# A feed-forward input turned by transposing transfers in place of TensorE's turns

## The chip, the cores and the metric

One core of one Trainium2 chip runs the whole program. The metric is the device time of one execution in microseconds (us). TensorE, VectorE, ScalarE and GpSimd work side by side, each following its own list of instructions and waiting on semaphores; transfers are issued from the queue of SyncE (SP).

## The reference, cut to what matters

The program computes one transformer layer: attention of x (4 x 2048 rows of 512) over a context of 4 x 154 rows, and then a quantised feed-forward part with a short convolution.

```python
x = x + xattn(layernorm(x), ctx)            # 16 heads of 32
h = bit_linear(layernorm(x), w1)            # act_quant of each row, ternary w1: 512 -> 2048
h = silu(depthwise_conv1d(h))               # 3 taps along the sequence
x = x + bit_linear(h, w2)                   # act_quant again, ternary w2: 2048 -> 512

def act_quant(x):
    scale = 127.0 / jnp.clip(jnp.max(jnp.abs(x), axis=-1, keepdims=True), 1e-05)
    return jnp.clip(jnp.round(x * scale), -128, 127) / scale
```

The change is about the input of the first `bit_linear`. Its rows are quantised with 128 sequence positions on the partitions, and the product with w1 needs the 512 channels there, so the quantised block must be turned (transposed).

## The kernel before

The 8192 rows are cut into 16 blocks of TB = 512 rows; a block is four tiles of P = 128 rows. Setup turns and splits the weights. Then 19 slots follow, numbered s = -1 to NB + 1 = 17 (`slots`, line 431). In slot s four blocks are under way: block s + 1 gets its first norm and queries (`do_q`), block s its attention, output projection, second norm and quantisation (`do_a`), block s - 1 its feed-forward part up to the quantised hidden layer (`do_f`), and block s - 2 its second product and result (`do_m`). Every engine's list is written out by hand in this order; there is no scheduler. "Slot 6" is s = 6, from about 595 to 680 us of the trace.

The step that changes stands at the end of a slot:

- ScalarE quantises the four tiles of block s (line 1522) into `osb`, as fp16 numbers; `hlq(i)` is the view of tile i, every second fp16 place of its 2 KB row. Each raises `xq_ok`.
- TensorE runs the 16 pieces of the query scores of block s + 1 (`query_scores`, line 1016). After each piece VectorE takes a maximum (line 1835); the banks alternate, so piece n waits for maximum n - 2. Between the pieces stand products of `mm2` (line 1085), and after pieces 13, 14 and 15 the turns `turn_xq` (line 1044): for each of four channel groups k, four transposes of 128 x 128 into half a PSUM bank (`xq_half`).
- ScalarE copies the four halves into `xqT` (line 1540), with the second copy of turned maxima `negmT` in between.
- TensorE turns the last maxima (line 1032), spreads the row of scales (`spread_row`, line 1053), and `mm1_ahead` (line 913) issues the first two products with w1 (line 891). The first of them waits for `xqc`, that is for the four copies. The next slot begins with the attention scores (line 854), which wait for the turned maxima that SP's queue brings into row 96 of `qs` (line 573, semaphore `m_in`).
- SP's list at the end of a slot: 12 transfers of the q parts (`qs<-hl`, line 558), two stores of border rows into `fx_scratch` (lines 565 and 566), two stores of results (line 511), the two transfers of turned maxima (line 573), each after its copy (`mtc`), two more stores of results, and then the load of x for a later slot (line 462).

In slot 15 there are no queries any more: the 16 turns stand together behind a part of `mm2(3)`, before the row of scales. `osb` is free for the next attention when the turns are over (line 1807), and for the border rows of the last step too (line 583).

Of the kernel before, what the change touches and what calls it, by code (L numbers as in the profile page):

```python
# [28 lines left out]
P = 128  # L29
# [9 lines left out]
def build(nc, x, ctx_in, Wq, bq, Wk, bk, Wv, bv, Wo, bo, w1, conv_w, conv_b, w2, out):  # L39
# [33 lines left out]
    with ExitStack() as ctx:  # L73
# [131 lines left out]

        def xq_half(s, k):

            bank = A[4] if k < 2 else A[5] if s == NB - 1 else F[0]
            return bank.bitcast(F16)[:, (k % 2) * TB:(k % 2 + 1) * TB]

        def row_bank(s):
# [11 lines left out]
        def hlq(i):  # L223

            return osb[:, i, :].bitcast(F16)[:, 0:2 * D:2]

# [94 lines left out]
        dgs_ok = sem("dgs_ok")  # L321
        xqt_ok = sem("xqt_ok")
        xqc = sem("xqc")
        sr_ok = sem("sr_ok")
# [121 lines left out]
        def _(sp):  # L446
# [59 lines left out]
            def slot(s, m, batch_of):  # L506
# [56 lines left out]
                if do_a:  # L563
                    sp.wait_ge(x2_ok, at(s, TT, TT))
                    sp.dma_start(fx_d[bass.ds(3 * s, 2), :], ring(s)[P - 2:P, TT - 1, :]).then_inc(fx_out[m % 2], 16)
                    sp.dma_start(fx_d[3 * NB:3 * NB + 1, :] if s == 0 else fx_d[bass.ds(3 * s - 1, 1), :],
                                 ring(s)[0:1, 0, :]).then_inc(fx_out[m % 2], 16)
                if do_m and do_a:
                    store_rows(range(2 if late_results(s) else TT))
# [10 lines left out]
                if s == NB:  # L580
                    for q in fx_out:
                        sp.wait_ge(q, 16 * NB)
                    sp.wait_ge(xqt_ok, KT * NB)
                    for bb in range(NBATCH):
# [110 lines left out]
        def _(pe):  # L695
# [135 lines left out]
            def slot(s, m, batch_of):  # L831
# [81 lines left out]
                def mm1_ahead(c):  # L913

                    if c == 0:
                        if s == 1:
                            pe.wait_ge(csum_ok, 1)
                        pe.wait_ge(xqc, at(s, KT, KT))
                        if do_m and s != NB - 1:
                            pe.wait_ge(out_ok, at(s, 4, 3 - 8))  # L920
                    if c == 1 and s == NB - 1:
                        pe.wait_ge(src, at(s, 1, 1))
                    mm1(c)

# [99 lines left out]
                def turn_maxima(tiles):  # L1024
# [8 lines left out]
                    r.then_inc(mt_ok, 1)  # L1033

                def turn_xq(ks):

                    for k in ks:
                        if k == 0:
                            pe.wait_ge(xq_ok, at(s, TT, TT))
                        if k == 2 and do_q:  # L1040
                            pe.wait_ge(mtc, at(s, 2, 3))
                        bank = xq_half(s, k)
                        for i in range(TT):
                            r = tp(bank[:, i * P:(i + 1) * P], hlq(i)[:, k * P:(k + 1) * P], identh[:])
                        r.then_inc(xqt_ok, 1)

# [124 lines left out]
                if s == NB - 1:  # L1171
                    mm2(2)
                    mm2(3, range(0, 11))
                    turn_xq(range(KT))
                    spread_row()
# [3 lines left out]
                for n in range(0 if s == NB - 1 else TT * NG):  # L1179
# [11 lines left out]
                    if do_q and n == 13:  # L1191
                        turn_maxima(range(0, TT - 1))
                    if do_a and n in (13, 14):
                        turn_xq((n - 13,))
                    if do_a and n == 15:
                        turn_xq((2, 3))
                if s == NB + 1:
# [22 lines left out]
        def _(act):  # L1220
# [73 lines left out]
            def slot(s, m, batch_of):  # L1294
# [242 lines left out]
                for k in range(KT):  # L1537
                    if do_a:
                        act.wait_ge(xqt_ok, at(s, KT, k + 2 - k % 2))
                        copy(xqT[:, k, :], xq_half(s, k)).then_inc(xqc, 1)  # L1540
                    if do_q and k == KT - 2:
# [15 lines left out]
        def _(dve):  # L1557
# [82 lines left out]
            def slot(s, m, batch_of):  # L1640
# [159 lines left out]
                def attention(k):  # L1800
# [5 lines left out]
                    elif k == 0:  # L1806
                        dve.wait_ge(xqt_ok, at(s, KT, 0))
                    dve.wait_ge(rz_ok, at(s, NG, k + 1))
# [238 lines left out]
```

## Time and profile before

| | us |
|---|---|
| median of 3 runs | 1520.56 (1520.53 to 1521.53) |
| the profiled execution | 1520.43 |
| its span, first to last instruction | 1518.6 |
| TensorE busy | 1460.6 (96%) |
| VectorE busy | 1278.0 (84%) |
| ScalarE busy | 1185.3 (78%) |
| GpSimd busy | 1028.7 (68%) |
| SP's queue, packets' share of 16 engines | 19.1% |

The profile is of one execution. Busy TensorE time is modelled from pipelined matmuls, each counted with its latency, so neighbours overlap and the share says less than it seems; which wait ended last is read from the timelines. In the rows PE is TensorE, DVE VectorE, ACT ScalarE, and SPq SP's queue; L1044 is line 1044 of the kernel. Copies on ScalarE all carry the line of the helper `copy`, L1222, and are told apart by their tiles. A row with x16 stands for 16 instructions merged, with the time from the start of the first to the end of the last.

### The profile page before, as it was taken

The numbers are of one execution on the slowest core, as the hardware profiler recorded it, in microseconds if no ns is written. First come the engines' busy times: TensorE is split into PE (matmuls) and PEld (weight loads), VectorE is DVE, ScalarE is ACT, GpSimd is POOL, SyncE is SP. The second block draws the span as 40 slices with busy tenths as digits, with TensorE's granted clock in tenths as the row PEclk, the third lists the DMA queues.
The fourth block names the chain that finished last, engine by engine and source line by source line (L and its number), as shares of the span: only waits on it lengthen the run. The fifth ranks groups of instructions, "written<-read, shape, count | busy, mean of one in ns | idle before, by whom it ended". The sixth has DMA issues, their size and how long they took to land. (4 is left out here: it accounts for less than half of the span.)

```text
span 1518.6 us, 24856 instructions
## 1 busy us (share of the span) xinstructions
PE 1460.6 (96%) x9102; PEld 892.5 (59%) x9102; DVE 1278.0 (84%) x2002; ACT 1185.3 (78%) x2190; POOL 1028.7 (68%) x834
## 2 busy tenths in 40 slices
PE   9998988999999999999999999999999999999898
PEld 6474655657575665657575665657575655656343
DVE  5787796898979889898979898897979898887877
ACT  3567788979787888979687888979687888978763
POOL 4011567868675977968675977968675877968543
PEclk8999899999999999999999999999999999999999
DMA  8561002021310303030310303030210202020001
GB/s 258 148 193 42 29 8 71 8 80 32 76 43 12 94 8 99 8 93 19 75 44 18 88 8 99 8 100 14 73 43 23 84 8 71 8 71 1 31 1 56
DMA packets 80343, 85.21 MB, mean 56 GB/s; under 512 B 29983, under 2 KB 55839, under 8 KB 79709
## 3 DMA queue, kind: packets, MB, share of 16 engines
q1 hardware_dynamic: 80221, 83.62, 19.1%
q8 instruction: 72, 1.18, 0.3%
q14 instruction: 50, 0.41, 0.1%
HBM read 38.74 MB, written 19.42 MB: 38 GB/s over the span
## 5 line engine op out<-in xcount | busy, mean ns | idle before, releaser
L675 POOL TENSOR_TENSOR h<-h,gall 128x512 f32<-128x512 f32 x233 | 343.9, 1476 | 18.3
L660 POOL TENSOR_TENSOR h<-h,r 128x512 f32<-128x512 f32 x240 | 307.0, 1322 | 52.5 <-ACT r L1222 50.6
L673 POOL TENSOR_TENSOR gall<-gall,cw 128x512 f32<-128x512 f32 x233 | 255.3, 1096 | 112.6 <-DVE h L1751 112.6
L1751 DVE SCALAR_TENSOR_TENSOR h<-gall,cw,h 128x512 f32<-128x512 f32 x249 | 253.2, 1020 | 47.6 <-ACT h L1320 47.4
L885 PEld LDWEIGHTS ps<-va,pexp 128*128 128x128 f32 x2048 | 259.5, 192 | 29.0 <-issue 10.9
L1676 DVE SCALAR_TENSOR_TENSOR gall<-ps,bias,srow 128x512 f32<-128x512 f32 x256 | 191.1, 747 | 94.3 <-POOL h L675 57.9
L891 PE MATMUL ps<-xqT,w1T 128*128 128x512 f16 x1024 | 255.1, 379 | 6.6 <-DVE gall L1676 6.5
L885 PE MATMUL ps<-va,pexp 128*128 128x33 f32 x2048 | 257.7, 270 | 0.0
L1085 PE MATMUL ps<-w2T,hqb 128*128 128x512 fp8e4 x960 | 242.4, 380 | 0.0
L1320 ACT ACTIVATE h<-gall,cb,cw 128x512 f32<-128x512 f32 x249 | 216.3, 869 | 8.3
L1301 ACT ACTIVATE pexp<-ps 128x512 f32<-128x512 f32 x320 | 179.8, 589 | 54.5 <-PE ps L854 27.9
L1835 DVE TENSOR_REDUCE negm<-ps 128x4 f16<-128x616 f32 x256 | 185.8, 793 | 20.3 <-PE ps L1016 15.0
L1222 ACT ACTIVATE hqb<-h 128x512 f16<-128x512 f32 x276 | 174.4, 683 | 36.0 <-POOL h L660 16.1
L710 PE MATMUL ps<-hl,WqT 128*128 128x512 f16 x768 | 170.8, 379 | 2.7 <-DVE hl L1793 2.6
L1339 ACT ACTIVATE h<-h 128x512 f32<-128x512 f32 x249 | 151.0, 688 | 12.3 <-POOL h L675 11.7
L997 PE MATMUL ps<-WoT,pexp 128*128 128x512 f16 x512 | 156.1, 382 | 1.7 <-DVE xn L1814 1.7
L891 PEld LDWEIGHTS ps<-xqT,w1T 128*128 128x128 fp8e4 x1024 | 101.8, 111 | 84.0 <-DVE gall L1676 8.9
L1085 PEld LDWEIGHTS ps<-w2T,hqb 128*128 128x128 f16 x960 | 92.5, 98 | 81.0 <-issue 3.9
L685 POOL TENSOR_TENSOR nw<-nw,mhalf 128x4 f32<-128x4 f32 x16 | 16.3, 1019 | 176.5 <-DVE nw L1845 176.5
L710 PEld LDWEIGHTS ps<-hl,WqT 128*128 128x128 f16 x768 | 74.1, 98 | 91.5 <-issue 8.0
L1016 PE MATMUL ps<-kB,hl 128*128 128x308 f16 x512 | 116.2, 305 | 11.5 <-DVE negm L1835 9.1
L1398 ACT ACTIVATE xn<-xr,sum 128x512 f32<-128x512 f32 x64 | 44.3, 717 | 78.0 <-DVE xr L1821 71.5
(226 smaller groups left out, 2336.8 us busy)
## 6 DMA issues: line engine op xcount, KB each, us to landing
qs<-hl SPq DMA_DIRECT2D x192, 128.0 KB, 2.4
xr<-in_x SPq DMA_DIRECT2D x16, 1024.0 KB, 5.4
out<-xr SPq DMA_DIRECT2D x64, 256.0 KB
h<-in_L_ffn_w SPq DMA_DIRECT2D x8, 1024.0 KB, 5.4
srow<-in_L_xattn_bo SPq DMA_DIRECT2D x15, 256.0 KB, 3.3
kst<-kh_scratch SPq DMA_DIRECT2D x32, 38.5 KB
xr<-in_ctx SPq DMA_DIRECT2D x1, 1024.0 KB
h<-in_L_xattn_Wk SPq DMA_DIRECT2D x1, 1024.0 KB, 8.2
```

What stands on the lines that cost most here:

```text
L660: gp.tensor_tensor(hc(c), hc(c), r2[:], ALU.mult).then_inc(u_ok, 1)
L673: gp.tensor_tensor(right, right, cw[:, c, 2:3].to_broadcast([P, TB]), ALU.mult).then_inc(c2m_ok, 1)
L675: gp.tensor_tensor(hc(c), hc(c), right, ALU.add).then_inc(c2p_ok, 1)
L710: r = mm(bank, a, b_, start=i == 0, stop=i == n - 1, **kw)
L885: r = mm(o, pr[:, t * P:(t + 1) * P], rhs, start=j == 0 and t % 2 == 0, stop=j == J, skip_group_check=True)
L891: r = mm(F[(c + 1) % 2], w1T[:, k, c * P:(c + 1) * P], xqT[:, k, :], start=k == 0, stop=k == KT - 1)
L1085: r = mm(bank, hq(c)[:, i * P:(i + 1) * P], w2T[:, c, :], start=False, stop=c == CT - 1, skip_group_check=late_results(s))
L1301: nc.scalar.activation(pexp[:, i % 3, :], A[i % 2], ACT.Exp, scale=1.0 / QS).then_inc(e_ok, 1)
L1320: nc.scalar.activation(hc(c), g[:, c % 4, 0:TB], ACT.Identity, bias=cb[:, c:c + 1], scale=cw[:, c, 0:1]).then_inc(c0_ok, 1)
L1676: ve.scalar_tensor_tensor(out=g[:, c % 4, 1:TB + 1], in0=F[(c + 1) % 2], scalar=bias1[:, c:c + 1], in1=srow[:], op0=ALU.add, op1=ALU.mult) ...
L1751: ve.scalar_tensor_tensor(out=hc(c), in0=g[:, c % 4, 1:TB + 1], scalar=cw[:, c, 1:2], in1=hc(c), op0=ALU.mult, op1=ALU.add).then_inc(c1_ok, 1)
L1835: ve.tensor_reduce(negm[:, i, k * J:(k + 1) * J].rearrange("p (b e) -> p b e", b=2), banks, AX.X, ALU.max, negate=True).then_inc(mx_ok, 1)
```

## The change

The four quantised tiles are turned by four transfers with `transpose=True`, issued on SP's queue in the slot of their block: transfer i waits for `xq_ok` of tile i and writes columns i * 128 to (i + 1) * 128 of all four channel groups of `xqT`. `turn_xq`, `xq_half`, the 64 copies and the semaphores `xqt_ok` and `xqc` are gone; `xq_turned` rises by 16 for each transfer. `hlq` is now a packed view. The first product waits for all four transfers, and the second one gets a wait for the first copy of turned maxima, which reads the bank that it writes.

```diff
--- before.py
+++ after.py
@@ -203,11 +203,6 @@
         def halves(bank, n):
             return bank.bitcast(F16)[:, 0:n]
 
-        def xq_half(s, k):
-
-            bank = A[4] if k < 2 else A[5] if s == NB - 1 else F[0]
-            return bank.bitcast(F16)[:, (k % 2) * TB:(k % 2 + 1) * TB]
-
         def row_bank(s):
 
             return F[0] if s == NB - 1 else A[2]
@@ -222,7 +217,7 @@
 
         def hlq(i):
 
-            return osb[:, i, :].bitcast(F16)[:, 0:2 * D:2]
+            return osb[:, i, :].bitcast(F16)[:, 0:D]
 
         def ah(k):
 
@@ -319,8 +314,7 @@
         pw2 = sem("pw2")
         xq_ok = sem("xq_ok")
         dgs_ok = sem("dgs_ok")
-        xqt_ok = sem("xqt_ok")
-        xqc = sem("xqc")
+        xq_turned = sem("xq_turned")
         sr_ok = sem("sr_ok")
         src = sem("src")
 
@@ -565,6 +559,10 @@
                     sp.dma_start(fx_d[bass.ds(3 * s, 2), :], ring(s)[P - 2:P, TT - 1, :]).then_inc(fx_out[m % 2], 16)
                     sp.dma_start(fx_d[3 * NB:3 * NB + 1, :] if s == 0 else fx_d[bass.ds(3 * s - 1, 1), :],
                                  ring(s)[0:1, 0, :]).then_inc(fx_out[m % 2], 16)
+                if do_a:
+                    for i in range(TT):
+                        sp.wait_ge(xq_ok, at(s, TT, i + 1))
+                        sp.dma_start(xqT[:, :, i * P:(i + 1) * P], hlq(i), transpose=True).then_inc(xq_turned, 16)
                 if do_m and do_a:
                     store_rows(range(2 if late_results(s) else TT))
                 if do_q:
@@ -580,7 +578,7 @@
                 if s == NB:
                     for q in fx_out:
                         sp.wait_ge(q, 16 * NB)
-                    sp.wait_ge(xqt_ok, KT * NB)
+                    sp.wait_ge(xq_turned, 16 * TT * NB)
                     for bb in range(NBATCH):
                         sp.dma_start(fxr[9 * bb:9 * bb + 9, :], fx_d[12 * bb:12 * bb + 9, :]).then_inc(fx_in, 16)
                         sp.dma_start(fx2[3 * bb:3 * bb + 3, :], fx_d[12 * bb:12 * bb + 9, :].rearrange("(m r) d -> m r d", r=3)[:, 1, :]
@@ -915,11 +913,13 @@
                     if c == 0:
                         if s == 1:
                             pe.wait_ge(csum_ok, 1)
-                        pe.wait_ge(xqc, at(s, KT, KT))
+                        pe.wait_ge(xq_turned, at(s, 16 * TT, 16 * TT))
                         if do_m and s != NB - 1:
                             pe.wait_ge(out_ok, at(s, 4, 3 - 8))
                     if c == 1 and s == NB - 1:
                         pe.wait_ge(src, at(s, 1, 1))
+                    if c == 1 and do_q:
+                        pe.wait_ge(mtc, at(s, 2, 3))
                     mm1(c)
 
                 def fix_turn():
@@ -1031,18 +1031,6 @@
                     for i in tiles:
                         r = tp(bank[0:H, i * P:(i + 1) * P], negm[:, i, :], identh[:])
                     r.then_inc(mt_ok, 1)
-
-                def turn_xq(ks):
-
-                    for k in ks:
-                        if k == 0:
-                            pe.wait_ge(xq_ok, at(s, TT, TT))
-                        if k == 2 and do_q:
-                            pe.wait_ge(mtc, at(s, 2, 3))
-                        bank = xq_half(s, k)
-                        for i in range(TT):
-                            r = tp(bank[:, i * P:(i + 1) * P], hlq(i)[:, k * P:(k + 1) * P], identh[:])
-                        r.then_inc(xqt_ok, 1)
 
                 def spread_row():
 
@@ -1171,7 +1159,6 @@
                 if s == NB - 1:
                     mm2(2)
                     mm2(3, range(0, 11))
-                    turn_xq(range(KT))
                     spread_row()
                     mm2(3, range(11, CT))
                     mm1_ahead(0)
@@ -1190,10 +1177,6 @@
                             mm2(3, MM2_LAST[n - 4])
                     if do_q and n == 13:
                         turn_maxima(range(0, TT - 1))
-                    if do_a and n in (13, 14):
-                        turn_xq((n - 13,))
-                    if do_a and n == 15:
-                        turn_xq((2, 3))
                 if s == NB + 1:
                     pe.wait_ge(out_ok, at(s, 4, 4 - 12))
                     for i in range(TT):
@@ -1535,9 +1518,6 @@
                         act.wait_ge(m_in, at(s, 32, 32))
                     copy(negmT[:, 0:LATE], halves(F[0], TB)[0:H, 0:LATE]).then_inc(mtc, 1)
                 for k in range(KT):
-                    if do_a:
-                        act.wait_ge(xqt_ok, at(s, KT, k + 2 - k % 2))
-                        copy(xqT[:, k, :], xq_half(s, k)).then_inc(xqc, 1)
                     if do_q and k == KT - 2:
                         act.wait_ge(mt_ok, at(s, 2, 4))
                         copy(negmT[:, LATE:TB], halves(A[0], TB)[0:H, LATE:TB]).then_inc(mtc, 1)
@@ -1804,7 +1784,7 @@
                         for q in v_out:
                             dve.wait_ge(q, 64)
                     elif k == 0:
-                        dve.wait_ge(xqt_ok, at(s, KT, 0))
+                        dve.wait_ge(xq_turned, at(s, 16 * TT, 0))
                     dve.wait_ge(rz_ok, at(s, NG, k + 1))
                     ve.tensor_tensor(osb[:, k, :].rearrange("p (u e d) -> p u e d", u=2, d=HD), opair(k)[:, :, :, 0:HD],
                                      rz[:, k].unsqueeze(3).to_broadcast([P, 2, 2 * J, HD]), ALU.mult).then_inc(at_ok, 1)
```

SP's queue at the end of slot 6, as its list stands before (`qs<-hl` are the q parts, `qs<-negmT` the turned maxima):

```order
L558 DMA qs<-hl 32x4x512 x12
L565 DMA fx_scratch<-xr 2x512
L566 DMA fx_scratch<-xr 1x512
L511 DMA out<-xr 128x512 x2
L573 DMA qs<-negmT 1x16x384
L573 DMA qs<-negmT 1x16x128
L511 DMA out<-xr 128x512 x2
```

and as it stands in the changed kernel:

```order
L552 DMA qs<-hl 32x4x512 x12
L559 DMA fx_scratch<-xr 2x512
L560 DMA fx_scratch<-xr 1x512
L565 DMA_TRANSPOSE xqT<-osb 128x4x128 x4
L505 DMA out<-xr 128x512 x2
L571 DMA qs<-negmT 1x16x384
L571 DMA qs<-negmT 1x16x128
```

The four transfers stand between the border rows and the first stores of results; all that follows on the queue is behind them.

TensorE at the end of the same slot before, from the 14th score piece on (L1016 the pieces, L1032 the turns of maxima, L1044 the turns that go, L1053 the row of scales, L891 the first two products):

```order
L1016 MATMUL ps<-kB,hl 128x308 x2
L1032 MATMUL ps<-identh,negm 16x128 x3
L1044 MATMUL ps<-identh,osb 128x128 x4
L1016 MATMUL ps<-kB,hl 128x308 x2
L1044 MATMUL ps<-identh,osb 128x128 x4
L1016 MATMUL ps<-kB,hl 128x308 x2
L1044 MATMUL ps<-identh,osb 128x128 x8
L1032 MATMUL ps<-identh,negm 16x128
L1053 MATMUL ps<-identf,qm 128x128 x4
L891 MATMUL ps<-xqT,w1T 128x512 x8
L854 MATMUL ps<-qs,kst 128x512 x3
```

and in the changed kernel:

```order
L1016 MATMUL ps<-kB,hl 128x308 x2
L1032 MATMUL ps<-identh,negm 16x128 x3
L1016 MATMUL ps<-kB,hl 128x308 x4
L1032 MATMUL ps<-identh,negm 16x128
L1041 MATMUL ps<-identf,qm 128x128 x4
L889 MATMUL ps<-xqT,w1T 128x512 x8
L852 MATMUL ps<-qs,kst 128x512 x3
```

The 16 turns are gone from between the pieces; the order of the rest is as before.

## Rows read from the trace of the kernel before

**Rows 1.** Groups of instructions, shapes apart: busy us, mean ns | idle before, releaser
```profile
L1222 ACT ACTIVATE xqT<-ps 128x512 f16<-128x512 f16 x64 | 34.4, 591 | 6.5 <-PE ps L1044 6.5
...
L1044 PE MATMUL ps<-identh,osb 128*128 128x128 f16 x256 | 23.4, 228 | 1.9 <-ACT osb L1522 1.9
```

**Rows 2.** VectorE in slot 6, in order of time: start us, us, what, count [idle]
```profile
663.79 11.47 DVE L1835 TENSOR_REDUCE negm<-ps 128x4 f16<-128x616 f32 x16 [0.70 <-PE ps L1016]
```

**Rows 3.** TensorE in slot 6, in order of time
```profile
674.11 0.61 PE L1044 MATMUL ps<-identh,osb 128*128 128x128 f16 x8
675.31 0.22 PE L1032 MATMUL ps<-identh,negm 128*16 128x128 f16 x1 [0.60 <-DVE negm L1835]
...
676.46 1.89 PE L891 MATMUL ps<-xqT,w1T 128*128 128x512 f16 x8
678.18 0.60 PE L854 MATMUL ps<-qs,kst 97*128 97x512 f16 x2
```

**Rows 4.** ScalarE in slot 6, in order of time
```profile
662.29 3.38 ACT L1522 ACTIVATE osb<-xr,qb,qm 128x512 f16<-128x512 f32 x4
...
675.74 0.57 ACT L1222 ACTIVATE xqT<-ps 128x512 f16<-128x512 f16 x1
```

**Rows 5.** SP's queue in slot 6, in order of time
```profile
668.51 0.25 SPq L566 DMA_DIRECT2D fx_scratch<-xr  x1
668.80 0.84 SPq L511 DMA_DIRECT2D out<-xr  x2
673.78 2.62 SPq L573 DMA_DIRECT2D qs<-negmT  x2
```

**Rows 6.** The transfers of turned maxima: issue ns min/median/max, then landing
```profile
L573 SPq DMA_DIRECT2D qs<-negmT x32: 538/566/587, 79.9 to 1357.8; - x32
...
DMA to landing us min/median/max: 1.7/2.0/3.7
```

**Rows 7.** DMA issues of the page: count, KB each, median us to landing
```profile
qs<-hl SPq DMA_DIRECT2D x192, 128.0 KB, 2.4
```

**Rows 8.** Three loads, line by line: issue ns min/median/max
```profile
L500 SPq DMA_DIRECT2D va<-v_scratch x4: 592/601/606, 66.4 to 1063.1; - x4
...
L455 SPq DMA_DIRECT2D cw<-in_L_ffn_conv_w x1: 3047/3047/3047, 6.7 to 6.7; - x1
...
L456 SPq DMA_DIRECT2D cb<-in_L_ffn_conv_b x1: 8817/8817/8817, 9.7 to 9.7; - x1
```

**Rows 9.** Slots 3 and 4: SP free, and the first product
```profile
412.40 0.24 SPq L566 DMA_DIRECT2D fx_scratch<-xr  x1
...
421.47 1.89 PE L891 MATMUL ps<-xqT,w1T 128*128 128x512 f16 x8
...
501.00 0.25 SPq L566 DMA_DIRECT2D fx_scratch<-xr  x1
...
507.74 1.46 PE L891 MATMUL ps<-xqT,w1T 128*128 128x512 f16 x6
```

**Rows 10.** Slots 0, 1 and 15: rows ready or SP free, and the first product
```profile
152.34 3.35 ACT L1522 ACTIVATE osb<-xr,qb,qm 128x512 f16<-128x512 f32 x4
...
160.28 1.89 PE L891 MATMUL ps<-xqT,w1T 128*128 128x512 f16 x8
...
237.40 0.25 SPq L566 DMA_DIRECT2D fx_scratch<-xr  x1
...
250.59 1.89 PE L891 MATMUL ps<-xqT,w1T 128*128 128x512 f16 x8
...
1426.57 3.37 ACT L1522 ACTIVATE osb<-xr,qb,qm 128x512 f16<-128x512 f32 x4 [0.90 <-DVE qb L1868]
...
1432.93 1.24 PE L891 MATMUL ps<-xqT,w1T 128*128 128x512 f16 x5
```

**Rows 11.** Two stretches of slot 1: us, TensorE busy (count), granted clock, DMA, GB/s
```profile
223.00:228.00 5.00, 1.11 (x14) 1.00 0.00 2
...
228.00:232.00 4.00, 3.84 (x30) 0.58 0.38 91
```

## Prediction

> **What bounds the kernel now.** I read the page first: TensorE is busy for 96% of the span, so at first sight every turn taken off it should pay. Then I read the groups of instructions for what is taken away: 256 turns (23.4 us of modelled time) and 64 copies on ScalarE (34.4 us) [rows 1]. Then the timelines of one slot, engine by engine, because a share of busy time doesn't say which wait ends last where the turns stand. The kernel has 16 slots that do this step; I take slot 6.
>
> From 663.79 to 675.26 VectorE runs 16 maxima with nothing between them [rows 2]. The turns are issued among the scores that feed them. The last eight start at 674.11 and are over at 674.72; then TensorE is idle for 0.60 us until the 16th maximum, turns the last maxima at 675.31, spreads the row of scales, and starts the first product of the feed-forward part at 676.46 and the first attention score at 678.18 [rows 3]. The last copy of xqT on ScalarE ends at 675.74 + 0.57 = 676.31, 0.15 before the product [rows 4]. So in slot 6 the end of the slot is set by the maxima, the last turn of them, and the row; turns and copies lie beside.
>
> SP's queue ends its second store into fx_scratch at 668.51 + 0.25 = 668.76, issues two stores of results (0.84), and waits until 673.78 for the turned maxima; it issues these two by 676.40 [rows 5]. Such an issue takes 0.57 and lands 2.0 after its start in the median [rows 6]: the second, issued at 676.40 - 0.57 = 675.83, lands at about 677.83, which is 0.35 before the score at 678.18 that needs it.
>
> **What is removed.** 16 turns a slot: their place is in TensorE's idle time under the maxima, so they give nothing in slots 2 to 14; TensorE merely waits longer at 675.31. If that cover were gone they would give at most 23.4 us in all. Four copies a slot on ScalarE (4 x 0.6): the last ends before the row's copy may start, so nothing is late that they held. The same goes for the packed output of the quantising activations: SP is not at that point when the rows are ready (in slot 6 they are done at 662.29 + 3.38 = 665.67 [rows 4], SP is free at 668.76). I cost all of this at 0.
>
> **What is added.** Four transposing transfers a slot on SP's queue, each of 128 rows of 512 fp16 numbers (128 KB), behind the stores into fx_scratch; a wait of the first product for all four; behind them on the same queue the two result stores, the two transfers of turned maxima, which the first attention score needs, and the next load of x. With t for the time that SP takes to issue one, the last is issued at start + 4t, and lands some 1.8 later: the transfer of q parts, also 128 KB, lands after 2.4 [rows 7], and I take 0.60 for its issue from the load of va [rows 8]. Nothing is lost while 4t + 1.8 fits between SP being free and the first product. That window is 676.46 - 668.76 = 7.70 in slot 6; 421.47 - 412.64 = 8.83 in slot 3, the longest of the 13 slots 2 to 14; 507.74 - 501.25 = 6.49 in slot 4, one of the shortest [rows 9]; the mean of the 13 is 7.56. The second way, over the turned maxima, gives nearly the same edge: 4t + 0.84 for the result stores + 0.57 for the first of the two + 2.0 to the landing of the second must fit into 678.18 - 668.76 = 9.42, so 4t up to 6.0, where the first way allows 5.9 in slot 6. One delay serves both.
>
> The edge is t = (7.56 - 1.8) / 4 = 1.44 us. The trace holds no transposing transfer, so t has to be bounded by other issues. Below: the load of va, 2048 pieces of 128 bytes, takes SP 0.60 us. Above: cw and cb, which are also 2048 pieces, but of 12 and 4 bytes, take 3.05 and 8.82 us [rows 8]. A transposing transfer has to break 1 KB rows into pieces that land on other partitions, so I expect it dearer than va and, since its pieces need not be as short as cw's, cheaper than cw. I take t = 2.0, a little above the middle of 0.60 and 3.05.
>
> The sum for t = 2.0: each of 13 slots loses 8.0 + 1.8 - 7.56 = 2.24, together 29.1. Slot 0: the first tile is ready a quarter of the four's 3.35 after 152.34, at 153.2, the last transfer lands at 153.2 + 9.8 = 163.0, against 160.28: 2.7. Slot 1: free at 237.65, product at 250.59, a window of 12.9: 0. Slot 15: the first tile is ready at 1427.4, landing 1437.2 against 1432.93: 4.3 [rows 10]. All together 36 us. A delay of this product is not given back later: the scores, the exponentials, the neighbours' copies and through them GpSimd's taps follow it in order. The profiled execution took 1520.43 us, 1.8 more than its span of 1518.6 and 0.1 less than the median of the runs; 1520.4 + 36 = 1556.
>
> By the same sum the bounds are: t = 0.60 gives 0, 1520; t = 1.4 loses only in the short slots and slot 15, 5 in all, 1526; t = 3.05 gives 13 x 6.44 + 7 + 1 + 9 = 101, 1621; t = 8.82 gives 13 x 29.5 + 30 + 24 + 32 = 470, 1990. Below nothing the bound is the whole of the turns, -23.
>
> **A second cost of waiting.** The granted clock fell in slot 1 to 0.58 of full on average from 228 to 232 (it is the lower of the two levels, 1.2 GHz, for most of that stretch), after TensorE had worked only 1.11 us of the 5 before [rows 11]. With a wait of some 4 us at the end of a slot TensorE would be as idle for as long, and what follows would run at half the clock for a stretch. I put this in the range, not in the sum, up to 4 x (1 - 0.58) = 1.7 us a slot.
>
> **What the skill says.** On the price of a transposing transfer the Trainium skill holds two rules that lead to opposite times, and no transfer of this trace tells which applies. "Advanced Engine Details and Errata", section "X-Bar Transpose (TRN2)", says that such transfers are as fast as regular ones; by that t is that of a plain 128 KB transfer, and the time stays at 1520. "VectorE: DVE Perf Modes", section "The three transpose paths", gives 1309 ns for one 128x128 block against 390 ns on TensorE; if a transfer here, which holds four such blocks, pays four times that, t is 5.2 and the time, as an estimate from that page, is near 1758.
>
> **The rivals.**
> First, in time: t stays under 1.4, as for va and the q parts, and every slot's window holds the four. For it: the 2048 pieces of va cost SP no more than the 16 of the turned maxima (0.60 and 0.57), and the queue has a hole of 4 us. Against it: cw and cb. It ends within 3 us of 1520: same. 0.24.
> Second, block by block: SP issues each 128x128 block as work of its own. Its price lies between cw and cb; their geometric middle is 5.2. Then each slot waits 4 x 5.2 + 1.8 - 7.56 = 15.0, 13 times 195, with 16, 10 and 17 for slots 0, 1 and 15: 238, or 1758. 0.20. The Trainium skill's price of a block, under "The three transpose paths" of "VectorE: DVE Perf Modes", would bring about the same.
> Third, on the other side: the turns do stand on the path. In slot 0 TensorE runs at the lower clock, and in all slots the turns stand before the scores 14 and 15, so that maxima might start later for them; if the transfers are in time and half of the 23.4 us is on the path, the time is 1509. Against it: the 16 maxima take 11.47 us, 0.717 each, with no gap [rows 2]. It can decide only where t is under 1.4. 0.05.
> The likeliest, t between 1.4 and 4: 0.51, with a range of its own from 1526 to 1682 (4 x 4 + 1.8 - 7.56 = 10.2 a slot, 161 in all).
>
> **How the numbers follow.** A measurement of this kernel can tell some 0.2%, 3 us, from no change. Faster 0.05, same 0.24, slower 0.71. The range must hold 8 in 10: it leaves out the faster case's far half and part of the second rival, and reaches from 1517 to 1735.
>
> **What would show it.** In slot 6 after: four transposing issues on SP's queue, 2 us each, directly behind the stores into fx_scratch; the first product waiting for a DMA into xqT, not for TensorE's own row; the transfer of turned maxima issued after 677 in place of 675.85; the maxima still 11.5 us; no gain in TensorE's stretch before. If the issues take 0.6 and the product starts 1.0 after the row, t was wrong and the first rival holds. If the time falls, the turns were on the path. If each issue is over 4 us, it is the second. If the clock falls once in each slot, the second cost of waiting is real.

## The result and the profile after

| | before | changed |
|---|---|---|
| median | 1518.99 us (1515.86 to 1524.08, 20 runs) | 1530.08 us (1520.56 to 1541.42, 20 runs) |
| the profiled execution, span | 1520.43, 1518.6 us | 1536.22, 1534.4 us |
| mean granted clock of that execution | 0.988 | 0.981 |

The ratio is 1.0069, with an interval from 1.0051 to 1.0088: slower, by some 11 us, where 36 were forecast. The changed kernel's profiled execution is the third slowest of its 20, so its rows show some 5 us more loss than the median has.

TensorE and ScalarE are relieved as the diff says. The page of the changed kernel, busy us (share) and instructions:

```profile
PE 1458.7 (95%) x8846; PEld 878.3 (57%) x8846; DVE 1290.1 (84%) x2002; ACT 1145.5 (75%) x2126; POOL 1021.9 (67%) x834
```

ScalarE has lost 40 us of work and TensorE only 2: the turns' 23.4 us are out, but part of the rest ran longer, at the lower clock. The two lines of transfers, the transposing ones and the turned maxima (columns as in [rows 6], with who waited for them: us, times):

```profile
L565 SPq DMA_TRANSPOSE xqT<-osb x64: 1215/1264/2578, 153.1 to 1448.7; - x64
...
  PE ps L889: 3.6, 3
...
DMA to landing us min/median/max: 2.3/2.4/4.4
```

```profile
L571 SPq DMA_DIRECT2D qs<-negmT x32: 533/584/1320, 79.8 to 1375.7; - x32
...
  PE ps L852: 4.1, 7
...
DMA to landing us min/median/max: 1.7/2.0/3.9
```

A transposing transfer takes SP 1.26 us to issue and lands 2.4 after the issue starts, 1.1 after it ends. The products with w1 waited for them three times only (slots 0, 12 and 15, for 0.32, 0.19 and 3.12); the attention scores waited seven times for the turned maxima. The 2.0 of the turned maxima is a median over two sizes: the first transfer of a slot, of 12 KB, takes 2.0 in the median and the second, of 4 KB, which is the one that a score waits for, 1.7, before and after.

Slot 6 is the slot read before. SP's queue, VectorE and TensorE in the changed kernel, in order of time, to be laid beside [rows 5], [rows 2] and [rows 3]:

```profile
677.66 0.25 SPq L560 DMA_DIRECT2D fx_scratch<-xr  x1
677.95 5.16 SPq L565 DMA_TRANSPOSE xqT<-osb  x4
683.15 1.05 SPq L505 DMA_DIRECT2D out<-xr  x2
684.25 1.22 SPq L571 DMA_DIRECT2D qs<-negmT  x2
```

```profile
672.93 11.39 DVE L1815 TENSOR_REDUCE negm<-ps 128x4 f16<-128x616 f32 x16 [0.73 <-PE ps L1016]
```

```profile
684.37 0.22 PE L1032 MATMUL ps<-identh,negm 128*16 128x128 f16 x1 [0.97 <-DVE negm L1815]
...
685.52 1.89 PE L889 MATMUL ps<-xqT,w1T 128*128 128x512 f16 x8
687.24 0.60 PE L852 MATMUL ps<-qs,kst 97*128 97x512 f16 x2
```

From the last turn of maxima to the first score it is 2.87 us, as before (678.18 - 675.31 = 2.87). The 16 maxima take 11.39 in place of 11.47: the turns among the scores had cost 0.08 a slot, about 1 us in all. TensorE's idle time before the last turn of maxima has grown from 0.60 to 0.97. In this slot the change costs nothing.

In slot 12 it does. SP's queue and TensorE:

```profile
1195.66 5.20 SPq L565 DMA_TRANSPOSE xqT<-osb  x4
...
1202.00 1.22 SPq L571 DMA_DIRECT2D qs<-negmT  x2
```

```profile
1200.50 0.22 PE L1032 MATMUL ps<-identh,negm 128*16 128x128 f16 x1 [0.97 <-DVE negm L1815]
...
1204.50 0.59 PE L852 MATMUL ps<-qs,kst 97*128 97x512 f16 x2 [0.60 <-DMA qs<-negmT]
```

The transposing transfers and the two result stores behind them hold SP until 1202.0. The second transfer of maxima is issued at 1202.6, 2.1 us after the last turn of maxima. In the kernel before, it is issued 0.54 after that turn in slot 6 (675.85 - 675.31), and the same in all the slots 1 to 14. In the changed kernel it is issued 0.8 to 2.1 after the turn in eight of the slots 2 to 14 (4, and 8 to 14).

In slot 4 a second thing comes on top. SP's queue and TensorE:

```profile
509.96 1.05 SPq L505 DMA_DIRECT2D out<-xr  x2
511.06 1.22 SPq L571 DMA_DIRECT2D qs<-negmT  x2
```

```profile
510.78 0.22 PE L1032 MATMUL ps<-identh,negm 128*16 128x128 f16 x1 [0.97 <-DVE negm L1815]
...
511.93 1.89 PE L889 MATMUL ps<-xqT,w1T 128*128 128x512 f16 x8
514.99 0.59 PE L852 MATMUL ps<-qs,kst 97*128 97x512 f16 x2 [1.17 <-DMA qs<-negmT]
```

The second transfer of maxima is issued at about 511.7, 0.9 after the last turn, and released the score at 514.99, 3.3 later, where 1.7 is the median landing. With a landing of 1.7 the score would not have waited. It comes 4.21 after the last turn of maxima, where it was 2.88 before. The two result stores, 256 KB each, stand directly ahead of the maxima here, but they aren't shown to be what makes this landing long: they stand there in slot 12 too, and in e8_order (below), which has no store in front, the landing in slot 4 is as long, from about 507.7 to 511.26:

```profile
505.70 2.56 SPq L564 DMA_DIRECT2D qs<-negmT  x2
```

```profile
507.18 0.22 PE L1030 MATMUL ps<-identh,negm 128*16 128x128 f16 x1
...
511.26 0.59 PE L850 MATMUL ps<-qs,kst 97*128 97x512 f16 x2 [1.44 <-DMA qs<-negmT]
```

Why a landing now and then takes some 3 us stays open; the kernel before has one too (slot 12, a wait of 0.43). Of the changed kernel's 4.1 us of waiting for maxima, 1.7 are two such landings (slots 4 and 7), 0.7 stand in slot -1, which has no transposing transfer, and the other 1.7 are in slots 9, 10, 12 and 14.

In slot 5 no transfer is late, and yet the end of the slot is stretched. TensorE in slot 5 of the changed kernel:

```profile
597.40 0.22 PE L1032 MATMUL ps<-identh,negm 128*16 128x128 f16 x1 [0.97 <-DVE negm L1815]
597.56 2.08 PE L1041 MATMUL ps<-identf,qm 128*128 128x128 f32 x8
599.42 2.68 PE L889 MATMUL ps<-xqT,w1T 128*128 128x512 f16 x8
601.94 0.60 PE L852 MATMUL ps<-qs,kst 97*128 97x512 f16 x2
```

The same eight row matmuls took 1.16 in slot 4. The windows around it (columns as in [rows 11]), first of the changed kernel, then of the kernel before at the same place of its slot 5:

```profile
583.00:590.00 7.00, 7.00 (x44) 1.00 0.77 183
590.00:597.50 7.50, 6.15 (x35) 1.00 0.52 122
597.50:601.00 3.50, 3.50 (x13) 0.51 0.74 282
```

```profile
576.60:583.60 7.00, 7.00 (x43) 1.00 0.66 158
583.60:591.10 7.50, 6.80 (x50) 1.00 0.47 138
591.10:594.60 3.50, 3.32 (x19) 1.00 0.40 151
```

Under the maxima TensorE works 6.15 of 7.5 us where it worked 6.80, and then the granted clock is 0.51 for 3.5 us: the lower level, 1.2 GHz. In both kernels slots 0 and 1 hold such stretches; behind them the changed kernel has four, at the ends of slots 5, 8 and 13 and in slot 15, and the kernel before two, at 1405.6 and 1487.5. Most of what the change adds stands in slots 0 and 1: from 140 to 260 us the mean granted clock is 0.84, where it was 0.91. From here on halved time is twice (1 - mean clock), times the execution; it is 58 us for the execution after and 36 for the one before.

The waits of TensorE that grew (us, times, longest), changed kernel first, then before:

```profile
PE ps L1032 <- DVE negm L1815: 15.5, 16, 1.1
PE ps L708 <- DVE hl L1773: 7.0, 10, 0.9
PE ps L852 <- DMA qs<-negmT: 4.1, 7, 1.2
```

```profile
PE ps L1032 <- DVE negm L1835: 8.9, 15, 0.7
PE ps L710 <- DVE hl L1793: 2.6, 5, 0.9
PE ps L854 <- DMA qs<-negmT: 1.0, 2, 0.6
```

The first pair costs no time by itself, since the maxima end when they end. The third is 3.1 us of late maxima. The second is a follow-up: in slots 5, 6, 9, 13 and 14, each behind the end of a slot that was delayed, VectorE's rows for the product with Wq come 0.9 late, 4.4 us more in all. That a delay shifts VectorE's list against TensorE's is my reading of it; nothing was run on it alone.

The 15.8 us between the two spans can be placed, from the last turn of maxima of one slot to that of the next, against the same stretch before:

| stretch of the changed kernel | us longer than before | what stands there |
|---|---|---|
| up to slot 2 | 4.2 | the lower clock in slots 0 and 1 |
| slots 6, 9 and 14 | 2.6 each, 7.8 | 3.4 us of lower clock at the start of each |
| slot 5 | 2.3 | a late score, 1.17, and no lower clock |
| slots 8, 10 and 13 | 0.7, 0.5, 1.4 | late scores, 0.51, 0.37 and 0.60 |
| the rest | -1.1 | |

Slot 5 has no lower clock at all, and is longer by twice its wait:

```profile
510.80:597.40 86.60, 82.63 (x504) 1.00 0.19 53
```

So a stretch of lower clock costs 1.7 us at once (from the last turn to the score it is 4.54 at the end of slot 5, in place of 2.87) and 0.9 by the follow-up. A late score costs its wait, and behind the two longest delays (at the ends of slots 4 and 12) the same 0.9.

### The profile page after: what moved, and what is told of

The parts are those of the page before. It is cut to its first block and busy times, and to the rows that moved or that the text cites. A ratio compares the mean times of both kernels' runs of the same rounds, so it can differ in the third digit from the quotient of the medians.

```text
span 1534.4 us, 24344 instructions
## 1 busy us (share of the span) xinstructions
PE 1458.7 (95%) x8846; PEld 878.3 (57%) x8846; DVE 1290.1 (84%) x2002; ACT 1145.5 (75%) x2126; POOL 1021.9 (67%) x834
## 3 DMA queue, kind: packets, MB, share of 16 engines
q8 instruction: 70, 1.15, 0.3%
## 5 line engine op out<-in xcount | busy, mean ns | idle before, releaser
L673 POOL TENSOR_TENSOR h<-h,gall 128x512 f32<-128x512 f32 x233 | 337.7, 1449 | 18.2
L1731 DVE SCALAR_TENSOR_TENSOR h<-gall,cw,h 128x512 f32<-128x512 f32 x249 | 263.2, 1061 | 49.0 <-ACT h L1303 48.6
L889 PE MATMUL ps<-xqT,w1T 128*128 128x512 f16 x1024 | 262.2, 387 | 7.8 <-DVE gall L1656 4.2
L1016 PE MATMUL ps<-kB,hl 128*128 128x308 f16 x512 | 117.3, 309 | 14.0 <-DVE negm L1815 11.9
L852 PE MATMUL ps<-qs,kst 97*128 97x512 f16 x256 | 95.6, 383 | 12.4 <-ACT pexp L1284 6.9
```

The source lines that it names most:

```text
L673: gp.tensor_tensor(hc(c), hc(c), right, ALU.add).then_inc(c2p_ok, 1)
L889: r = mm(F[(c + 1) % 2], w1T[:, k, c * P:(c + 1) * P], xqT[:, k, :], start=k == 0, stop=k == KT - 1)
L1731: ve.scalar_tensor_tensor(out=hc(c), in0=g[:, c % 4, 1:TB + 1], scalar=cw[:, c, 1:2], in1=hc(c), op0=ALU.mult, op1=ALU.add).then_inc(c1_ok, 1)
```

## The experiments

Every kernel was timed beside the kernel before on the same chip. "Halved" is the halved time defined above, the mean over its runs. The ratios don't follow the medians alone; where the two say different things both are given.

| kernel | median us (range, runs) | ratio to before (interval) | halved |
|---|---|---|---|
| changed kernel | 1530.08 (1520.56 to 1541.42, 20) | 1.0069 (1.0051 to 1.0088) | 57.1 |
| e1_fill | 1531.83 (1525.92 to 1538.02, 6) | 1.0077 (1.0053 to 1.0102) | 49.0 |
| e2_stores | 1528.32 (1517.04 to 1531.22, 12) | 1.0044 (1.0025 to 1.0063) | 53.2 |
| e3_both | 1519.55 (1516.18 to 1526.46, 12) | 0.9999 (0.9987 to 1.0012) | 39.3 |
| e4_row | 1514.63 (1512.83 to 1525.95, 7) | 0.9967 (0.9955 to 0.9979) | 44.2 |
| before, with e1 to e4 | 1519.99 (24) | | 40.5 |
| e5_nothing | 1523.31 (1519.2 to 1530.71, 12) | 1.0020 (1.0007 to 1.0033) | 53.9 |
| e6_unused | 1527.07 (1523.75 to 1539.25, 9) | 1.0053 (1.0028 to 1.0077) | 48.3 |
| e7_fill_only | 1520.36 (1517.76 to 1525.61, 11) | 0.9999 (0.9988 to 1.0010) | 43.7 |
| e8_order | 1516.48 (1511.87 to 1528.98, 12) | 0.9984 (0.9964 to 1.0004) | 50.1 |
| before, with e5 to e8 | 1520.11 (32) | | 41.4 |
| e9_row_warm | 1515.29 (1511.62 to 1520.28, 11) | 0.9981 (0.9969 to 0.9992) | 41.1 |
| e10_before_stores | 1519.27 (1516.23 to 1524.41, 12) | 1.0004 (0.9991 to 1.0016) | 38.0 |
| before, with e9 and e10 | 1518.62 (23) | | 37.1 |

**e1_fill** is the changed kernel with 16 turns on TensorE at their old places, into banks that nobody reads:

```diff
+                    if do_a and n in (13, 14):
+                        turn_unused((n - 13,))
+                    if do_a and n == 15:
+                        turn_unused((2, 3))
```

> The changed kernel, with the 16 turns back on TensorE at their old places in slots 0 to 14; their results are read by nobody, xqT still comes from the transposing transfers, and ScalarE's copies stay away. Theory 'clock' (the turns kept TensorE busy under the maxima; without them the granted clock falls to half after the end of some slots, 1.7 us and more each): no halved stretch at the end of slots 5, 8 and 13, shorter ones in slots 0 and 1, and a time 5 to 8 us under the changed kernel's 1530, near 1523. Theory 'queue' (only SP's later transfers cost time): 1530, as without the turns, since SP's queue is the same. If the turns stood on the path, 1530 + 10 or more.

The idle time before the last turn of maxima is back where it was, but the maxima are still late. TensorE's waits in e1_fill:

```profile
PE ps L1033 <- DVE negm L1833: 8.7, 15, 0.7
...
PE ps L853 <- DMA qs<-negmT: 2.9, 6, 1.1
```

Halved time fell from 57 to 49, the time didn't: 1531.83, where the theory of the clock said 1523. So the turns by themselves don't buy the loss back while the queue is as the change left it.

**e2_stores** is the changed kernel with the result stores behind the turned maxima:

```diff
-                if do_m and do_a:
-                    store_rows(range(2 if late_results(s) else TT))
                 if do_q:
...
-                if late_results(s):
-                    store_rows(range(2, TT))
+                if do_m and do_a:
+                    store_rows(range(TT))
```

> The changed kernel, with the first two result stores of a slot issued behind the two transfers of turned maxima in place of before them. Theory 'queue': the waits of the first attention score for the turned maxima (4.1 us in 7 slots) go, with the delay of 1.0 us that follows one in the next slot where it is long: 5 us less, near 1525. Theory 'clock' alone: 1530, the halved stretches stay.

No score waits for the maxima any more; that row is gone from the waits. The time hardly moved: the median is 1528.32, where 1525 was expected, and the interval of the ratio overlaps that of the changed kernel. Halved time is 53. Slot 4 of e2_stores, windows on TensorE:

```profile
505.00:507.00 2.00, 0.76 (x5) 1.00 0.38 84
507.00:511.00 4.00, 4.00 (x15) 0.57 0.55 207
```

With nothing waiting for a transfer there, TensorE works 0.76 of the last 2 us under the maxima, and then runs at 0.57. The other slots from 2 to 14 of this trace have the same idle time and keep the higher level.

**e3_both** is e1_fill and e2_stores together.

> Both edits together: turns kept, read by nobody, and the result stores behind the turned maxima. If clock and queue together are the whole loss: within 3 us of the kernel before, 1517 to 1522, the waits of the score for a DMA under 1.5 us in all. If something else costs time too: over 1524.

1519.55, the time of the kernel before, with its halved time too (39.3 beside 40.5). Both together take back the whole loss, and no third thing is needed. In slot 4 of e3_both SP issues the maxima directly behind the transposing transfers, and the score follows the last turn of maxima by 3.00 us:

```profile
508.42 1.22 SPq L570 DMA_DIRECT2D qs<-negmT  x2
```

```profile
508.30 0.22 PE L1031 MATMUL ps<-identh,negm 128*16 128x128 f16 x1 [0.59 <-DVE negm L1831]
...
511.30 0.60 PE L851 MATMUL ps<-qs,kst 97*128 97x512 f16 x2
```

**e4_row** takes e2_stores and spreads the row of scales before the last turn of maxima, into a bank that the turns have left free:

```diff
-            return F[0] if s == NB - 1 else A[2]
+            return F[0] if s == NB - 1 else A[4]
...
+                    if do_a and n == 15:
+                        pe.wait_ge(xq_ok, at(s, TT, TT))
+                        spread_row()
```

> The changed kernel with the stores behind the turned maxima, and the four products that spread the row of scales moved ahead of the turn of the last maxima, into the bank that the turns no longer use. They fill TensorE's idle time under the last maxima (about 1.0 of 1.2 us), and the first product of the next part starts 1.0 us earlier in each slot. The score still waits for the turned maxima, which land 0.35 us before it in the kernel before, so I expect 0.3 us a slot of gain beside the loss that goes: 1513 to 1518 by 'clock' and 'queue' together, with few halved stretches. If the clock does not care for this filling: 1520 to 1525.

The lowest median of all: 1514.63, 0.9967 of before, from 7 runs. Its profiled execution is the slowest of them, 1525.95, by one stretch at the lower clock that is shown under e6_unused. TensorE in slot 6 of e4_row:

```profile
680.59 1.05 PE L1039 MATMUL ps<-identf,qm 128*128 128x128 f32 x8
681.72 0.22 PE L1030 MATMUL ps<-identh,negm 128*16 128x128 f16 x1
682.47 1.89 PE L887 MATMUL ps<-xqT,w1T 128*128 128x512 f16 x8 [0.53 <-DVE xr L1855]
```

The row's 1.05 us lie under the last maximum now. The product starts 0.75 after the last turn of maxima in place of 1.15 (685.52 - 684.37 in the changed kernel), and what holds it is VectorE, which has still to read the bank that it writes. 0.4 in each of 14 or 15 slots is 6 us, the gain over before is 5. Against e2_stores, from which it differs by the row alone, the gain is 14 by the medians and 12 by the ratios, more than the 6: the row also fills TensorE's idle time under the maxima, 7.04 us of 7.5 busy here in place of 6.15.

**e5_nothing** takes the turns out and puts no transfers in, except in slot 0:

```diff
-                if do_a:
+                if s == 0:
                     for i in range(TT):
...
-                        pe.wait_ge(xq_turned, at(s, 16 * TT, 16 * TT))
+                        pe.wait_ge(xq_ok, at(s, TT, TT))
```

> The changed kernel, with the transposing transfers of slot 0 alone; in slots 1 to 15 xqT keeps the rows of block 0, and TensorE waits for the quantised tiles instead of the transfers (the results of later blocks are those of other data). So TensorE's turns and ScalarE's copies are gone and SP's queue is as short as before the change. Theory 'clock': the granted clock falls in some slots as in the changed kernel, about 53 us of halved clock in place of 40, and the time is 1524 to 1527, over the kernel before although work is gone and nothing is waited for. If only the queue costs: 1520 or a little under.

**e7_fill_only** is e5_nothing with the unread turns of e1_fill.

> As e5_nothing, with the 16 turns back on TensorE in slots 0 to 14, their results read by nobody. ScalarE's copies are gone, and SP's queue is short. Theory 'clock': back to 1518 to 1521 with some 40 us of halved clock, so more work on TensorE and less time than e5_nothing; the difference to e5_nothing is the whole price of the missing turns. If the copies on ScalarE were worth anything: under 1517.

Neither has the queue's work, and their difference is the turns alone: 1523.31 without, 1520.36 with them, halved time 53.9 and 43.7. The work of 16 turns a slot costs nothing, and taking it out costs some 3 us (1 to 5, by drawing anew from the runs of both). e7_fill_only also lacks the 64 copies on ScalarE, and is as fast as the kernel before (0.9999, interval 0.9988 to 1.0010): the copies are worth nothing that shows. TensorE in the 3.5 us behind the last turn of maxima of slot 0, e5_nothing and then e7_fill_only:

```profile
158.00:161.50 3.50, 2.92 (x11) 0.50 0.27 59
```

```profile
159.20:162.70 3.50, 3.49 (x19) 1.00 0.43 63
```

In the traces of all twelve kernels this place tells the two sorts apart. Without turns or row under the maxima (changed kernel, e2_stores, e5_nothing) the 3.5 us are at 0.50 to 0.57 in 5 of 6 cases in slots 0 and 1 and in 4 of 39 in slots 2 to 14. With the 16 turns, read or unread (before, e1_fill, e3_both, e6_unused, e7_fill_only, e10_before_stores), they are never under 0.85 in slots 0 and 1 and always at 1.00 in the 78 cases of slots 2 to 14; with the row moved there (e4_row, e8_order, e9_row_warm) at 1.00 in all 39. In e5_nothing's trace it is slots 0 and 1 alone that pay.

**e6_unused** is the kernel before, turns and copies in place, with the four transposing transfers a slot added, into a half of `osb` that nobody reads:

```diff
+                if do_a:
+                    for i in range(TT):
+                        sp.wait_ge(xq_ok, at(s, TT, i + 1))
+                        sp.dma_start(xqU[:, :, i * P:(i + 1) * P], hlq(i), transpose=True).then_inc(xq_turned, 16)
```

> The kernel before, with turns and copies in use, and beside them the four transposing transfers of a slot on SP's queue at the place of the changed kernel, into a half of osb that nobody reads (the quantised tiles packed as in the changed kernel). Theory 'queue': the turned maxima are late as in the changed kernel, the first score waits for them in about 6 slots, 3 us in all, with a delay behind some of them in the next slot: 1523 to 1528. Theory 'clock': the halved stretches stay near those of the kernel before, save where the wait itself brings one. If the queue costs nothing: 1520.

1.0053, 7 us, from the added transfers alone: the product doesn't wait for them, only the maxima stand behind them. Its waits show six scores held by the maxima:

```profile
PE ps L861 <- DMA qs<-negmT: 2.6, 6, 0.6
```

2.6 us of waiting doesn't make 7. Halved time is 48.3 beside 41.4; at the 0.4 us of time per halved us that the changed kernel's own runs show (slope 0.39 over its 20 runs) that is some 3 us more. In the profiled execution, 9.1 us longer than that of the kernel before, 7.8 us are lost at one place: from the last turn of maxima of slot 5 at 591.78 to that of slot 6 it is 92.2 us in place of 84.4, with TensorE at the lower clock for 14 us:

```profile
597.50:611.50 14.00, 14.00 (x56) 0.51 0.22 76
```

It begins 2 us after a score that waited 0.58. e4_row's profiled execution has the same at the same place (8.0 us lost, from 595 on), behind a score that waited 1.19. Other late scores are followed by nothing of the kind, the 1.17 in slot 4 of the changed kernel among them, and what sets off such a long stretch is not shown.

**e8_order** is e4_row with the border rows, too, behind the turned maxima: the queue runs transposing transfers, maxima, border rows, results.

> The changed kernel with the row of scales spread ahead of the turn of the last maxima (into the bank that the turns left), and on SP's queue the transposing transfers directly behind the q parts, then the turned maxima, and only then the stores of border rows and results. In e4_row the first product waited 8.0 us in 7 slots for the last transfer, 0.3 to 0.9 a slot; here it is issued 0.75 us earlier. I expect 1511 to 1514, 2 us under e4_row at equal clock. If the first score and not the first product sets the slot: as e4_row, 1514 to 1516.

1516.48, over the 1511 to 1514 that were expected, and not told apart from e4_row by these runs (0.9984, interval up to 1.0004). In e4_row's trace the seven waits of the first product for a transfer are 0.56 to 1.07 in six slots and 3.14 in slot 15 (the expectation has them too small); e8_order's trace keeps two, in slots 0 and 15. So the waits in between can go without the time falling.

**e9_row_warm** is e4_row with 8 unread turns, behind pieces 13 and 14.

> e4_row with 8 of the 16 turns back on TensorE, read by nobody, behind the score pieces 13 and 14, so that TensorE has under the last maxima about what it had before the change: 8 turns and the row of scales in place of 16 turns. Theory 'clock': halved clock back to some 40 us (e4_row 44, e8_order 50), and the row's gain stays: 1512 to 1515, with fewer runs over 1520 than e8_order had. If the halved stretches of e4_row and e8_order come from something else, such as the waits of the first product for the last transfer: 1515 to 1518 and 45 to 50 us halved.

1515.29, halved time 41.1, just outside the 1512 to 1515 expected by 'clock'. Its slowest of 11 runs is 1520.28, where e4_row had 1525.95 and e8_order 1528.98; its ratio, 0.9981, is no better than e4_row's.

**e10_before_stores** is the kernel before with its result stores behind the turned maxima.

> The kernel before, with the first two result stores of a slot issued behind the turned maxima, as in e3_both. A control: in the kernel before SP's queue has time for them in front, so theory 'queue' expects no change, 1518 to 1521, and e3_both owes nothing to the move but the loss it takes back. If the move is a gain by itself (the maxima land sooner without stores in front of them): 1515 to 1518.

1.0004: the order of the stores is worth nothing where no transposing transfers stand ahead of them. So e3_both owes its time to having undone the change's own damage, not to an improvement of the kernel before.

## Why the prediction was right and wrong

**The step that failed.** The forecast of 36 us was a sum of waits of the first product for the transposing transfers, 29.1 of it in slots 2 to 14, from an issue of t = 2.0 us. The issue measured 1.26, and in those 13 slots the product waited once, 0.19 us. The 11 us came from two steps that were costed at 0: the removal of the turns, which lets the granted clock fall, and the turned maxima that stand behind the transfers on the queue. The direction, slower, was right for a reason that did not hold.

**The removed work is worth nothing on the path: right.** The maxima bound the end of the slot, before and after (11.47 and 11.39 us), and e7_fill_only shows the copies at nothing. The third rival, turns on the path, had at most 1 us of truth in it, 0.08 a slot. That the removal costs time by the clock is another matter, below.

**t, the issue of one transposing transfer: the mis-sized term.** It was taken as 2.0 and measures 1.26. That lies between the bounds and under the edge of 1.44, in the first rival's country. With it and the measured landing, 5.2 + 1.1 = 6.3 fits even into the 6.49 of slot 4, and the prediction's own sum falls from 36 to about 1. It would have said 1521, and would have missed the 11 us. The choice of 2.0 rested on va as the lower and cw as the upper row and the middle between them; the measured value is nearer to va. Of the two rules, the Trainium skill's "Advanced Engine Details and Errata", section "X-Bar Transpose (TRN2)", agrees with the landing (2.4 us, that of a plain 128 KB transfer in [rows 7]) and not with SP's time, which is twice the 0.6 of va. The 1309 ns that the Trainium skill's "VectorE: DVE Perf Modes", section "The three transpose paths", gives for a block is near the 1.26, but for four blocks of 128 x 128 here, not for one; the second rival, which priced by the block, is refuted.

**Slot 0 and slot 15.** Of slot 0's 2.7 us 0.3 came as a wait. Slot 15's 4.3 came to nothing although its product waits 3.12 us for the transfers, because VectorE reads that product only after other work. TensorE and VectorE in slot 15 of the changed kernel:

```profile
1451.10 3.48 PE L889 MATMUL ps<-xqT,w1T 128*128 128x512 f16 x8 [3.12 <-DMA xqT<-osb]
```

```profile
1454.94 1.39 DVE L1656 SCALAR_TENSOR_TENSOR gall<-ps,bias,srow 128x512 f32<-128x512 f32 x2
```

VectorE starts on it 10.96 us after the quantising begins at 1443.98; before it was 10.99, from 1426.57 [rows 10].

**"One delay serves both": wrong.** The edge of the maxima path, 4t up to 6.0, was worked out for slot 6 alone, and there it holds: 4t is 5.2 and nothing is late. In slots 9, 10, 12 and 14 SP is free later against the end of the maxima, and the score waits for the maxima while the product waits for nothing, or 0.19 in slot 12. The landing was also taken as 2.0, the median of both sizes, where the one that counts has 1.7; that made the slack in slot 6 look like 0.35 us where it is some 0.6. The product path was costed and the maxima path waved through; it was the maxima path that lost, 3.1 us of waiting in the profile beyond the 1.0 before, and with what follows from it up to the 7 us of e6_unused, where no product waits for a transposing transfer.

**The second cost of waiting: put in the wrong place.** I tied the lower clock to a wait of 4 us behind late transfers, and kept it out of the sum. It came with no wait for any transfer: the change's own removal makes TensorE idle under the maxima (6.15 busy of 7.5, where it was 6.80), and the clock falls in slots 0 and 1 and at the ends of some later slots, not of each. It belongs to the step "what is removed", which I costed at 0. e5_nothing against e7_fill_only puts it at 3 us, e2_stores against e3_both at 9 by the medians and 7 by the ratios.

**What stays open.** The two causes don't add up. With both, 1530.1; with the queue alone, 1531.8 (e1_fill) and 1527.1 (e6_unused); with the turns alone gone, 1528.3 (e2_stores, transfers in place) and 1523.3 (e5_nothing, none); with neither, 1519.6. With the transfers in place either one brings most of the loss. A late score and missing turns both leave TensorE idle at the same place, and that both end in the lower clock would explain it, but it isn't shown; e1_fill's halved time is lower than the changed kernel's and its time is not, and slot 5 of the changed kernel loses 2.3 us at the full clock, so the clock isn't all of it. What makes single landings and single stretches at the lower clock long is open too. Nor is it settled why the stretches at the lower clock fall in some slots and runs and not in others: the 20 runs of the changed kernel spread over 21 us, those of the kernel before over 8.

## What to carry to other kernels

Work hidden under another engine isn't free to remove: on TensorE it can be what keeps the granted clock up, and a pair of kernels with and without unread turns showed that (3 us for 23 us of work that was on no path). When transfers are added to a queue, follow each one already on it to its consumer, in every slot and not in one; the small, urgent ones go ahead of large stores. What a moved step really gives back may be its buffer: the PSUM bank that the turns left let the row of scales go under the last maximum. With the stores moved behind the maxima as well, that made the changed kernel faster than the one before (1514.6 beside 1520.0); with the stores moved alone it was 1528.3.

## What the runs showed of the hardware

- A transposing transfer from SBUF to SBUF, 128 rows of 512 fp16 numbers, takes its queue 1.26 us in the median (1.22 to 2.58), four in a row 5.16 to 5.24 in slots 0, 4 and 6, 5.76 in slot 8, and lands 2.4 us after its issue begins (2.3 to 4.4).
- A transfer of 4 KB of turned maxima lands 1.7 us after its issue begins in the median; in slot 4 it released its reader only after 3.3, with two stores of 256 KB issued just ahead of it, and in e8_order after 3.5 with none.
- In slot 5 of the changed kernel the clock was at its lower level for 3.5 us after 7.5 us in which TensorE had been busy for 6.15; other slots with the same list of instructions kept the higher one. Over the 20 runs of the changed kernel each us of halved time went with 0.39 us of time; the stretches of 3.4 us at the ends of slots 5, 8 and 13 cost 2.6 us each.
- Sixteen transposes a slot on TensorE, read by nobody, took the mean halved time from 53.9 to 43.7 us (e5_nothing, e7_fill_only).
